# A four-layer graph network kernel on one core: the order of every engine's steps and the banks of its product tiles, laid out anew

## The reference, cut to what matters

```python
h = maximum(layernorm(x), 0); x = x + L0(h, adj)   # attention, scores by the nodes' pair index, softmax over rows
h = maximum(layernorm(x), 0); x = x + L1(h, adj)   # attention, layernorm, sum over adj, an MLP of two layers
h = maximum(layernorm(x), 0); x = x + L2(h, adj)   # attention, softmax over columns, elu
h = maximum(layernorm(x), 0); x = x + L3(h, adj)   # fixed 512x512 softmax matrix made of adj and the edge values e
```

## Time and profile before

| | us |
|---|---|
| median of 3 runs | 1015.85 |
| lowest, highest | 1012.22, 1019.29 |
| span of the profiled execution | 1013.8 |
| PE busy | 949.6 (94%) |
| DVE busy | 859.2 (85%) |
| ACT busy | 632.5 (62%) |
| POOL busy | 555.4 (55%) |

### The profile page before, as it was taken

One profiled execution on the slowest core, in us unless ns is written; L12 is line 12 of the kernel. 1 busy time (PEld: TensorE's weight loads), 2 busy tenths in 40 slices (PEclk: granted clock), 3 DMA queues, 4 the chain that ended last, 5 costly groups with the idle time before them and its releaser, 6 DMA issues. The chain is left out here.

```text
span 1013.8 us, 21212 instructions
## 1 busy us (share of the span) xinstructions
PE 949.6 (94%) x7355; PEld 902.1 (89%) x7355; DVE 859.2 (85%) x2526; ACT 632.5 (62%) x1655; POOL 555.4 (55%) x1171
## 2 busy tenths in 40 slices
PE   5989999999999999999999999998999999997998
PEld 4779998988998889899989899998999898886897
DVE  5988897989979988977888888799988989779874
ACT  3347547686668653775686664877548584677741
POOL 3535264582575652765566565654636744467850
PEclk9978999999999999999999999999999999999999
DMA  5020000000020010011000101101000100000003
GB/s 135 1 63 1 1 2 1 2 1 1 2 83 2 1 43 2 1 37 49 2 1 2 43 1 43 43 2 33 11 1 2 42 2 2 21 1 2 1 1 105
DMA packets 38071, 19.99 MB, mean 20 GB/s; under 512 B 3142, under 2 KB 37452, under 8 KB 37964
## 3 DMA queue, kind: packets, MB, share of 16 engines
q1 hardware_dynamic: 36080, 18.42, 6.5%
q10 hardware_dynamic: 1884, 0.21, 0.2%
HBM read 10.23 MB, written 8.39 MB: 18 GB/s over the span
## 5 line engine op out<-in xcount | busy, mean ns | idle before, releaser
L686 PE MATMUL ps<-HE,PT 128*128 128x129 f32 x2048 | 238.5, 276 | 3.2 <-issue 1.9
L686 PEld LDWEIGHTS ps<-HE,PT 128*128 128x128 f32 x2048 | 233.1, 192 | 5.4 <-issue 4.8
L451 ACT ACTIVATE Y<-X,SM 128x128 f32<-128x128 f32 x512 | 204.0, 491 | 49.3 <-POOL SM L447 49.1
L1307 DVE SCALAR_TENSOR_TENSOR PT<-ps,CE,maskT 128x512 f32<-128x512 f32 x256 | 174.2, 742 | 19.2 <-PE ps L810 11.8
L432 POOL TENSOR_TENSOR SM<-ST 128x8 f32<-128x8 f32 x96 | 29.5, 307 | 269.4 <-DVE ST L1170 269.3
L443 POOL TENSOR_TENSOR SM<-SM,minus_half 128x8 f32<-128x8 f32 x96 | 163.3, 1701 | 7.6
L686 PE MATMUL ps<-W,HT 128*128 128x128 f32 (+1 forms) x768 | 126.1, 311 | 0.0
L686 PEld LDWEIGHTS ps<-W,HT 128*128 128x128 f32 x768 | 115.6, 193 | 8.9
L1170 DVE BATCH_NORM_STATS2 ST<-X 128x6 f32<-128x128 f32 x512 | 104.8, 278 | 3.1 <-DMA X<-in_x_dram 0.4
L703 PE MATMUL ps<-ident,Y 128*128 128x128 f32 x640 | 85.6, 278 | 10.7 <-ACT Y L451 10.2
L703 PEld LDWEIGHTS ps<-ident,Y 128*128 128x128 f32 x640 | 72.2, 143 | 16.3 <-ACT Y L451 14.4
(11 more groups left out here) (260 smaller groups left out, 2335.6 us busy)
## 6 DMA issues: line engine op xcount, KB each, us to landing
X<-in_x_dram SPq DMA_DIRECT2D x32, 256.0 KB, 3.5
out_dram<-X SPq DMA_DIRECT2D x32, 256.0 KB, 2.8
adj_raw<-in_adj_dram SPq DMA_DIRECT2D x4, 256.0 KB, 3.5
W<-in_L_gnn_W_dram SPq DMA_DIRECT2D x2, 64.0 KB, 3.8
W<-in_L_gnn_W_dram SPq DMA_DIRECT2D x1, 128.0 KB, 3.6
bias<-in_L_gnn_bias_dram SPq DMA_DIRECT2D x2, 64.0 KB, 4.1
Wo<-L_gnn_others_weight_dram ACTq DMA_DIRECT2D x1, 64.0 KB, 3.1
feat1w<-in_L_gnn_Wp_dram ACTq DMA_DIRECT2D x1, 64.0 KB, 3.5
```

What stands on the lines that cost most here:

```text
L451: a = nc.scalar.activation(dst[:, n, 0:F], src[:, n, 0:F], func, scale=SM[s][:, S_RSTD, n:n + 1], bias=SM[s][:, S_SHIFT, n:n + 1])
L686: return nc.tensor.matmul(o, w, m, start=start, stop=stop, skip_group_check=True)
L1307: a = V.scalar_tensor_tensor(out=PT[r][:, j, :], in0=o, scalar=CE[s][:, c:c + 1], in1=maskT[:, j, :].bitcast(F32), op0=ALU.max, op1=ALU.mult)
```

## The change

Only the strings `TURNS` (all five engines) and `HOMES` differ. Every string has the same letters as often as before, so each engine does the same steps. One line of each, before and after, the rest being of the same sort:

```diff
 TURNS = {
-    "pe": ("gggg0110101020g2120012413240303410101033114040511522553305120232123223032304143130550100001110404151"
...
+    "pe": ("gggg1001010220g1102012314320403104101313010041412525353502025213213034202312410330050351040110104114"
...
-HOMES = ("0123456701234567012347056123412341235641702356415670415067125304304356717204356072071241207431256074"
...
+HOMES = ("0123456710234567102345671023471023471563024756356021356012536470647061253247061746174270427503754203"
```

More of the change, by code:

```diff
@@ L136 @@
-    "pool": ("01201043120153240135234010521430510021421562374626234736847783865384547989a596a96755a679ab67687b87bc"
-           "ab98da89c8adbcae9cdde9ebc9ebdabfcfafefdcdfcebfdefcdbecfdefef"),
-    "sp": ("403510617228394a5b6c7d8e9fadcbef"),
-}
-HOMES = ("0123456701234567012347056123412341235641702356415670415067125304304356717204356072071241207431256074"
[L141 to L148, removed]
@@ new lines @@
+    "pe": ("gggg1001010220g1102012314320403104101313010041412525353502025213213034202312410330050351040110104114"
+           "2412515440545055202151321222342642226367676743467262373233433443473467648486488657687635767838757578"
+           "3848584885495598999655699a56a6959a9799769aa9767665a566a5767767877a87ba7ba68bba9ab68a6a7b8b7889878ba8"
+           "bab8cb989cadbdcbda9ccb8989dd989caca9a9a9aaddaececebcacbeecdcdceded9b9bdd9edebebebcebefcfbeffafbdbdcf"
+           "bfacafdffcffdcfcfcececcdcfdddfededdffbeedeeffffebfeebeffcdfcdcedfefef"),
@@ new lines @@
+    "dve": ("g120gggg0101g20g010310140012115322043041100321104312322503033154122054523134200324415301025350012100"
+            "4541100141545215105432203514612425372242262627667633646426377237334348743767448563483688678745478887"
+            "355763888948654769598999a5699955a76659595a9798aa9a6767a566a58a69767b676877a7ba9ba7a678b8bb6abbb78c8a"
+            "9a788bdab8b899c8dc8badccab89cd9d89ccc9a9adeadb9aaebdec9dc9caeceebdcdeeed9bbdc9adeecfebabdefbfdcffbbf"
+            "edfbffaccebffaffdcdecfbccffeccddfdeeccffddededffebdeefefefefcffdbcdefef"),
@@ new lines @@
+    "act": ("g12010g120g01334204011300112450011530012012504322130103312120502304031014121104245520405154022311355"
+            "41232452236426543723764462723234733434644688376684573638757655348787548845679896578599656a6a69985697"
+            "976a59797a6566587977a7687a8bb9686a8ab796a7b8a877a9ba888b9acabb9cad8da9c98bdb8c8999aadbcaaaeebc9bcecd"
+            "db9ecacdb9bd9cdebedcbeebdcfebfcabdfefdcacdbeadffdcfcffefcccedffebdfedfdcedffeebfdfeeefffbdcecdcfedef"
+            "fef"),
+    "pool": ("1200103140213542013235401025410510302142156237462637247368478385438546795989a6965a75a976a7b68b678b7a"
+             "b9c8ad9c88cda9bcdeade9eb9cebdfabfcafedfcdfbcefedfbecfdcdeeff"),
@@ new lines @@
+    "sp": "503401617228394a5b6c7d8e9fabcdef",
+}
+HOMES = ("0123456710234567102345671023471023471563024756356021356012536470647061253247061746174270427503754203"
+         "7542375370536701105367105432761276051423760512376405127360546464056124703562412724031567272574031631"
+         "5407263263726154037261542604260374125603417256025602534170265341702653174651702346467051467056714023"
+         "4203425671073107423516234075165176517234065140653472472414720653147204724706531702431657065724315067"
+         "2431350135031503015306724301672430152467301524624567301526734016753240342340167523401675234061752175"
+         "2173406173541720672067207635416735167365174203651367420513674274260517346025172517342603451726034725"
+         "1036053125476310251012525470631256347012502501634706325251256314701470256371431402756315653165365364"
+         "0271536402157364021420573675365365367531426037501475301265347012653470126570121342165703432142143657"
+         "0214536720134654365437206154061561403720320375614562037145623710623062371062371062306457123064571")
```

## The result

The changed kernel takes 1042.86 us (median of 4 runs, 1038.6 to 1043.4), against 1014.78 for the kernel before beside it: a ratio of 1.027 with a 95% interval of 1.024 to 1.030. It is 28 us slower. I had forecast 1007, with 5% for slower by more than 1%. What follows says where the 28 us are and which sentence of the prediction let them in.

A forecast was written before the change was run, and what follows sets the result against it. TensorE was taken as the bound, busy 949.6 of 1013.8 us. Middle -5.5, clock -1.5, head 0 and tail -2 gave 1004.8; with 2.0 for the timed median, 1007 us, range 998 to 1017.

The forecast's parts named there:

- the order's trips: TensorE fills a tile, ScalarE or VectorE reads it, TensorE waits for the result; 240 counted, 47 lacking cover before, 35 after.
- the cover: TensorE work standing inside such a round trip; what was missing was to fall from 28.1 us to 19.6.
- The sum: Whole kernel: -5.5 - 1.5 + 0 - 2 = -9.0 us on the profiled execution, 1013.8 to 1004.8.
- the head: Early steps: one TensorE wait goes, another for LOW takes its time; 0 us, bounds -3 and +2.
- the middle: 105 to 850 us: shorter TensorE waits, 8.6 us counted, two thirds taken, -5.5; bounds 0 and 16.0.
- The clock: Middle: low-clock stretches behind waits of group 9 may go, 0 to 3.0 us; 1.5 taken.
- the tail: Late groups: a shorter VectorE run and earlier statistics of group e gain 2 us, bounds 0 and 4.
- The rule: VectorE instructions with two SBUF inputs and GpSimd ones reading SBUF block one another; weighed in the tail, 1.6 us.
- gin1: Slower rival: the chain from att1b to gin1 has 46 us of cover, not 52, and starves; 1031, chance 0.07.
- The two stretches named: Middle, group 9: TensorE at 1.2 GHz behind the waits for cmax0 and spread1a, each costing some 1.5 us.
- DVE paces: Rival: waits only move to where VectorE is behind, the tail alone is won; 1014, chance 0.23 shared with another clock fall.

The follow-up runs named there:

- the fills: Changed order with GpSimd's four wide instructions replaced by fills that read nothing: 1010.8 us; the order before with the same fills: 1007.8 us.
- a_head_scale: Changed order with group 2's layer norm put back behind group 0's (stat0 on VectorE and GpSimd, scale0 on ScalarE): 1042.8 us, ratio 1.028.

## Why the prediction was wrong, point by point

- *"Each engine has the same steps with the same instructions, so all durations stay."* This is the sentence that failed. The durations of DVE and POOL instructions hang on what the other engine does at that moment: 13.6 us of stalls became 39.0, and without them 25 of the 28 us are gone. I counted the order's trips with fixed lengths; cmax0 of group 9 got the cover that I counted, and its trip grew by L1185's 1.9 us and by the `LOW` held in front of it.
- *The sum fails without the stalls too.* With the fills the changed order was still 3 us slower, where the sum said 9 faster. On the profiled executions with fills the head is +6.5 against 0 in the sum, the middle with its clock -15 against -7, the tail +9.5 against -2. Head and tail are terms of waits, mis-sized because trip lengths, queues of DVE, ACT and POOL and the places of their steps were taken as fixed.
- *The rule was in the text and used once.* I weighed it for the single pair L1342 and L1125 in the tail, as 1.6 us. I should have asked how often a wide POOL instruction can meet a two-input DVE instruction in each order. Of the named rivals none was this one; the slower one, gin1, did not come (all its waits for its `LOW` come to 0.7 us).
- *The middle, -5.5.* With the fills it is -15, the clock included, near the upper bound of 16 and well above the 8.6 counted. With the real instructions it is +12 (from 7.5 behind to 20). The count had the direction right, and the stalls took back 27 us. Single trips were wrong even so: spread1a of group 9 waited for ACT's queue, with the fills too.
- *The clock, -1.5.* The two stretches named are gone, but there are fifteen in place of seven, with 82 us at the lower level in place of 41. It came with the waits. By PE's pitches, an estimate, about half of the 28 us is lost in such stretches (34 us against 18) and half as idle time; with the fills it was 27 against 20.
- *The head, 0 (bounds -3 and +2).* It is about +8, outside both bounds, and nearly as much with the fills. I wrote that agg0's `LOW` "came just as late"; it ended at 79.37 against 70.71. I had compared only DVE's steps near it and not when ACT's rows and PE's own earlier steps let them begin.
- *The tail, -2.* It is +8: norm2 of c and e wait 4.3 and 3.4 us. I had looked at e and f alone, and not at c, whose statistics moved behind self0 and feat3 on DVE. The step that I called deciding, feat2 of f, waited 1.68 us in place of 0.75.
- *DVE paces* was the rival nearest to the truth, priced at 1014 as a gain that doesn't come. I gave it no way to make DVE itself slower. The rival with the nearest number was gin1, 1031, but what it describes did not happen; had the time fallen on it, that would have been luck.

## What to carry to other kernels

Before an order is laid out with durations from a trace, mark the pairs that exclude one another, here DVE with two SBUF inputs (or a copy or `TENSOR_SCALAR` in SBUF) and any POOL instruction that reads SBUF; a wide one holds up the smallest, and a fill still holds up the copy or `TENSOR_SCALAR`. If an engine's busy time changes while its instruction count does not, look there first, and replace the suspects by fills of the same length: the gap between the two kernels then shows what the meeting costs. In an order as tight as this one, do not trust a count of covers or an edit at one place: moving one step back cured its own wait and opened others.

## What the runs showed of the hardware that I had not expected

- In the changed kernel 29 DVE instructions with two SBUF inputs, or copying or scaling from SBUF, began inside a wide POOL one, 0.2 us or more before its end, and all 29 were held. The 18 small ones (8 elements, 0.17 us alone) ended 21 to 33 ns behind POOL's, up to 2.1 us late; the 11 wide ones ended 1.08 us behind it.
- It goes both ways: 128x8 POOL instructions of 0.2 us took 1.06 to 1.19 us while DVE ran wide ones with two SBUF inputs.
- A POOL copy of 128x1024 took 1.04 us (median), the addition of two such tiles 2.37 to 2.39 (medians of L1130 and L1125), and two whole fills and a half 2.4.
- Executions repeat almost instruction for instruction: after a_head_scale's edit at 35 us PE ran 1.3 to 1.8 us ahead of the changed kernel at every point between 149 and 924 us.
